# Moving dt's four columns onto z's projection, and the steps of one block's work, in an attention and Mamba kernel on one Trainium2 core

## What is computed

```python
# layer 0
q = einsum('dc,bcn->bnd', wq, xf) + bq; k = einsum('dc,bcn->bdn', wk, xf) + bk[:, None]
attn = softmax(einsum('bnd,bdm->bnm', q, k), axis=-1)
x = gamma * einsum('bcn,bmn->bcm', v, attn) + x            # v likewise
# layer 1
u = layernorm(x as tokens) * norm_g + norm_b
zxbcdt = u @ in_w.T                                        # 256 z, 512 xBC, 4 dt
z, xBC, dt = split(zxbcdt); dt = softplus(dt + dt_bias)
xBC = silu(causal depthwise conv of 4 taps over xBC + conv_b); xs, Bm, Cm = split(xBC)
state = state * exp(dt * A) + (dt * xs) Bm                 # 4 heads of 64, state 128, over tokens
y = (state . Cm + Dp * xs) * silu(z)
out = rmsnorm(y) * rms_w @ out_w.T
x + out * sigmoid(se2 @ relu(se1 @ mean(out) + se1_b) + se2_b)
```

## Time and profile before

| | |
|---|---|
| median of 3 runs | 3152.42 us (3150.59 to 3152.76) |
| the profiled execution | 3150.87 us, its span 3148.70 us |
| PE busy | 2980.0 us, 95% |
| PEld busy | 2322.5 us, 74% |
| DVE busy | 2032.0 us, 65% |
| ACT busy | 1930.0 us, 61% |
| POOL busy | 2009.9 us, 64% |
| mean granted clock of TensorE | 0.983 |

### The profile page before, as it was taken

How to read it: one execution, slowest core, us unless ns; L and a number is a source line. 1 busy time by engine, 2 the same in 40 slices (tenths; PEclk the granted TensorE clock), 3 DMA queues, 4 the chain that set the end, 5 groups by cost and what they waited for, 6 DMA issues and landing times. The chain is left out here.

```text
span 3148.7 us, 63156 instructions
## 1 busy us (share of the span) xinstructions
PE 2980.0 (95%) x21208; PEld 2322.5 (74%) x21208; DVE 2032.0 (65%) x3417; ACT 1930.0 (61%) x3742; POOL 2009.9 (64%) x3087
## 2 busy tenths in 40 slices
PE   6899999999999999999999999999999999999984
PEld 3767777777777777777777777777777777777762
DVE  5556666666666676676676666676666667666654
ACT  2565666666656566666665666666666666666652
POOL 2446666667756576666676656666676667777753
PEclk9999999999999999999999999999999999999986
DMA  3111111111311121222221222122221111212121
GB/s 123 49 37 46 44 51 58 31 54 49 103 63 65 58 71 58 91 77 74 82 77 38 72 76 72 62 76 69 65 89 36 43 49 55 69 50 69 42 95 67
DMA packets 101970, 200.99 MB, mean 64 GB/s; under 512 B 18480, under 2 KB 41392, under 8 KB 97264
## 3 DMA queue, kind: packets, MB, share of 16 engines
q1 hardware_dynamic: 98192, 195.08, 18.6%
q10 hardware_dynamic: 3456, 1.86, 0.2%
HBM read 131.21 MB, written 64.75 MB: 62 GB/s over the span
## 5 line engine op out<-in xcount | busy, mean ns | idle before, releaser
L723 POOL TENSOR_TENSOR p_lo<-p,p_hi 128x512 f16<-128x512 f32 x1024 | 1221.9, 1201 | 845.6 <-ACT p_hi L886 711.9
L879 ACT ACTIVATE p<-p_et 128x512 f32<-128x512 f32 x1024 | 612.2, 598 | 637.4 <-PE p_et L1138 598.0
L1156 PE MATMUL acc<-v_hi,p_hi 128*128 128x257 f16 x4096 | 954.3, 273 | 4.0 <-DVE work L1464 3.8
L1158 PE MATMUL acc<-v_lo,p_hi 128*128 128x256 f16 x4096 | 951.8, 272 | 0.0
L1420 DVE TENSOR_REDUCE maxes<-p_mx 128x1 f32<-128x1024 f32 x508 | 620.1, 1221 | 489.1 <-PE p_mx L1117 488.7
L886 ACT ACTIVATE p_hi<-p 128x512 f16<-128x512 f32 x1024 | 643.5, 629 | 10.0
L1164 PE MATMUL acc<-v_hi,p_lo 128*128 128x257 f16 x4096 | 622.8, 274 | 15.1 <-POOL p_lo L723 15.1
L1156 PEld LDWEIGHTS acc<-v_hi,p_hi 128*128 128x128 f16 x4096 | 399.3, 97 | 125.0 <-issue 54.8
L1158 PEld LDWEIGHTS acc<-v_lo,p_hi 128*128 128x128 f16 x4096 | 400.6, 98 | 117.8 <-issue 49.9
L1164 PEld LDWEIGHTS acc<-v_hi,p_lo 128*128 128x128 f16 x4096 | 399.9, 98 | 68.0 <-POOL p_lo L723 15.9
L1138 PE MATMUL p_et<-qs,kst 98*128 98x256 f16 x2048 | 393.3, 273 | 11.6 <-ACT p L879 11.1
(11 more groups left out here) (213 smaller groups left out, 4164.2 us busy)
## 6 DMA issues: line engine op xcount, KB each, us to landing
work<-rows_d SPq DMA_DIRECT2D x32, 1024.0 KB, 5.2
xin<-in_x_dram SPq DMA_DIRECT2D x48, 512.0 KB, 4.7
xr<-in_x_dram SPq DMA_DIRECT2D x32, 512.0 KB, 3.8
x_d<-x1c SPq DMA_DIRECT2D x31, 512.0 KB, 2.9
og_d<-og SPq DMA_DIRECT2D x29, 512.0 KB, 2.7
mix_x<-x_d SPq DMA_DIRECT2D x25, 512.0 KB, 4.7
mix_o<-og_d SPq DMA_DIRECT2D x24, 512.0 KB, 5.5
out_dram<-mix_o SPq DMA_DIRECT2D x24, 512.0 KB, 2.8
```

Source lines behind the costliest of these rows:

```text
L723: e.tensor_tensor(p_lo[:, n % RING, :], p32[:, n % P32S, :], p_hi[:, n % RING, :], ALU.subtract).then_inc(lo_pool, 1)
L879: e.activation(p32[:, n % P32S, :], p_et[:, :], ACT.Exp).then_inc(exp_done, 1)
L1156: e.matmul(acc[:, t, 0:C + 1], p_hi[:, r, at:at + P], v_hi[:, 2 * k + kk, 0:C + 1], start=(k == 0 and kk == 0), stop=False)
L1158: e.matmul(acc[:, t, 0:C], p_hi[:, r, at:at + P], v_lo[:, 2 * k + kk, :], start=False, stop=False, skip_group_check=True)
```

## The change

- dt has no fill of its own. z is made in four fills of one chunk each, 260 columns wide: 256 of z and dt's 4. Its weights lie in a tensor of their own, inz_sb, loaded with two DMAs; inT_sb keeps the 512 columns of the convolution.
- z's fills are at steps 10, 11, 13 and 15. ScalarE takes the tanh and VectorE adds dt's bias and makes the product, chunk by chunk, in the same steps. zt has two buffers, by block parity, and outputs wait for their own chunk only.
- dt's further work starts at step 15 (K_DT): VectorE 15 and 17, ScalarE 16, softplus on GpSimd 18 to 21, dA still at K_DAT-2, now 22, dAT 24, cumT and decay_rows 26.
- The convolution is at steps 12, 17, 22, 27; the first xsB at 26; the second xT at 19 in place of 30, and with it the next load of xr; the first yn at 26.
- In VectorE's step max_parts is issued right behind the maxima, ahead of stage_b and stage_a.

The diff, cut to its core:

```diff
@@ -47,20 +47,20 @@
 
 
 
-K_X1T, K_UT, K_DT, K_DAT, K_CUM, K_YT, K_OUT = 2, 9, 10, 21, 23, 30, 0
+K_X1T, K_UT, K_DT, K_DAT, K_CUM, K_YT, K_OUT = 2, 9, 15, 24, 26, 30, 0
 K_U = (6, 7)
-K_XBC = (11, 16, 21, 26)
-K_Z = (22, 24)
-K_XSB = (25, 27, 28, 29)
+K_XBC = (12, 17, 22, 27)
+K_Z = (10, 11, 13, 15)
+K_XSB = (26, 27, 28, 29)
 K_SRC = (1, 5, 9, 13)
 K_CB = (2, 6, 10, 14)
 K_Y = (4, 8, 12, 17)
 K_SUM = (6, 10, 14, 19)
 K_SQ = (8, 12, 16, 21)
-K_XT = (13, 30)
+K_XT = (13, 19)
 K_XB = 4
 K_RMS = 22
-K_YN = (27, 28)
+K_YN = (26, 28)
 K_LN = 1
 K_BN = 20
 
...
@@ -128,15 +128,13 @@
             out += [("x1T", A, 0), ("x1T", A, 1)]
         if K == K_UT:
             out += [("uT", A, 0), ("uT", A, 1)]
-        if K == K_DT:
-            out += [("dt", A, 0)]
         if K == K_DAT:
             out += [("dAT", A, 0)]
         if K == K_CUM:
             out += [("cumT", A, 0)]
-        for r in range(2):
-            if K == K_Z[r]:
-                out += [("z", A, r)]
+        for t in range(QT):
+            if K == K_Z[t]:
+                out += [("z", A, t)]
         for c in range(QT):
             if K == K_XSB[c]:
                 out += [("xsB", A, c)]
...
-        inT_sb = sb("inT_sb", [P, CH, 2 * C + 2 * NST + NH])
+        inT_sb = sb("inT_sb", [P, CH, CONVD])
+        inz_sb = sb("inz_sb", [P, CH, C + NH])
...
-        zt = work[:, 5120:6144].rearrange("p (t c) -> p t c", t=QT)
+        zt0 = work[:, 5120:6144].rearrange("p (t c) -> p t c", t=QT)
...
+        zt = [zt0, sb("zt1", [P, QT, C])]
...
-                   (inT_sb[:, :, :], inT.rearrange("(h p) n -> p h n", p=P)),
+                   (inT_sb[:, :, :], inT[:, C:C + CONVD].rearrange("(h p) n -> p h n", p=P)),
+                   (inz_sb[:, :, 0:C], inT[:, 0:C].rearrange("(h p) n -> p h n", p=P)),
+                   (inz_sb[:, :, C:C + NH], inT[:, C + CONVD:C + CONVD + NH].rearrange("(h p) n -> p h n", p=P)),
...
-                e.wait_ge(zs_done, 2 * g + 2)
+                e.wait_ge(zs_done, QT * g + c + 1)
...
@@ -949,13 +950,12 @@
                         e.wait_ge(conv_done, n + 1)
                         wait(e, silu_done, n - 1)
                         e.activation(th[:, m % 2, :], cv, ACT.Tanh).then_inc(tanh_done, 1)
-                for r in range(2):
-                    if K == K_Z[r]:
-                        key = ("z", g, r)
+                for t in range(QT):
+                    if K == K_Z[t]:
+                        key = ("z", g, t)
                         e.wait_ge(filled, n_filled(key))
-                        wait(e, y_ready, g * QT)
-                        e.activation(zt[:, 2 * r:2 * r + 2, :], bank(key)[:, :].rearrange("p (t c) -> p t c", t=2),
-                                     ACT.Tanh, scale=0.5).then_inc(ztanh_done, 1)
+                        wait(e, y_ready, (g - 1) * QT)
+                        e.activation(zt[g % 2][:, t, :], bank(key)[:, 0:C], ACT.Tanh, scale=0.5).then_inc(ztanh_done, 1)
                 for c in range(QT):
                     if K == K_XSB[c]:
                         key = ("xsB", g, c)
...
@@ -1194,20 +1194,12 @@
                 elif name == "uT":
                     e.wait_ge(u_done, 2 * g + 2)
                     turn(key, u, i)
-                elif name == "dt":
+                elif name == "z":
                     e.wait_ge(uT_done, 2 * g + 2)
                     o = begin(key)
-                    for t in range(QT):
-                        for h in range(CH):
-                            mm = e.matmul(o[:, t * NH:(t + 1) * NH], uT[:, h, t * P:(t + 1) * P],
-                                          inT_sb[:, h, C + CONVD:C + CONVD + NH], start=(h == 0), stop=(h == CH - 1))
-                    mm.then_inc(filled, 1)
-                elif name == "z":
-                    o = begin(key)
-                    for t in range(2):
-                        for h in range(CH):
-                            mm = e.matmul(o[:, t * C:(t + 1) * C], uT[:, h, (2 * i + t) * P:(2 * i + t + 1) * P],
-                                          inT_sb[:, h, 0:C], start=(h == 0), stop=(h == CH - 1))
+                    for h in range(CH):
+                        mm = e.matmul(o[:, 0:C + NH], uT[:, h, i * P:(i + 1) * P], inz_sb[:, h, :],
+                                      start=(h == 0), stop=(h == CH - 1))
                     mm.then_inc(filled, 1)
                 elif name == "dAT":
                     o = begin(key)
...
@@ -1487,24 +1479,6 @@
-                if K == K_DT:
-                    key = ("dt", g, 0)
-                    e.wait_ge(filled, n_filled(key))
-                    wait(e, dt_ready, g)
-                    v.tensor_tensor(dtt[:, 0, :].rearrange("p (t h) -> p t h", h=NH),
-                                    bank(key)[:, 0:TH].rearrange("p (t h) -> p t h", h=NH),
-                                    dtb[:, :].unsqueeze(1).to_broadcast([P, QT, NH]), ALU.add).then_inc(dtin_done, 1)
...
@@ -1529,13 +1503,27 @@
                         v.tensor_copy(xbc[:, :, 0:HALO], xbc[:, :, BLK:BLK + HALO]).then_inc(halo_done, 1)
                     else:
                         v.memset(xbc[:, :, 0:HALO], 0.0).then_inc(halo_done, 1)
-                for r in range(2):
-                    if K == K_Z[r]:
-                        key = ("z", g, r)
-                        e.wait_ge(ztanh_done, 2 * g + r + 1)
-                        v.scalar_tensor_tensor(zt[:, 2 * r:2 * r + 2, :], zt[:, 2 * r:2 * r + 2, :], 1.0,
-                                               bank(key)[:, :].rearrange("p (t c) -> p t c", t=2), ALU.add, ALU.mult)\
-                            .then_inc(zs_done, 1)
+                for t in range(QT):
+                    if K == K_Z[t]:
+                        key = ("z", g, t)
+                        e.wait_ge(ztanh_done, QT * g + t + 1)
+                        if t == 0:
+                            wait(e, dt_ready, g)
+                        v.tensor_tensor(dtt[:, 0, t * NH:(t + 1) * NH], bank(key)[:, C:C + NH], dtb[:, :], ALU.add)
+                        v.scalar_tensor_tensor(zt[g % 2][:, t, :], zt[g % 2][:, t, :], 1.0, bank(key)[:, 0:C],
+                                               ALU.add, ALU.mult).then_inc(zs_done, 1)
+                if K == K_DT:
+                    e.drain()
+                    v.scalar_tensor_tensor(dtt[:, 1, :], dtt[:, 0, :], -1.0, dtt[:, 0, :], ALU.mult, ALU.max)\
+                        .then_inc(dtabs_ready, 1)
+                    v.tensor_scalar(dtt[:, 3, :], dtt[:, 0, :], 0.0, None, ALU.max)
+                if K == K_DT + 2:
+                    e.wait_ge(dtexp_done, g + 1)
+                    v.tensor_scalar(dtt[:, 4, :], dtt[:, 2, :], 2.0, None, ALU.add)
+                    e.drain()
+                    v.reciprocal(dtt[:, 5, :], dtt[:, 4, :])
+                    e.drain()
+                    v.tensor_tensor(dtt[:, 4, :], dtt[:, 2, :], dtt[:, 5, :], ALU.mult).then_inc(dtz_ready, 1)
                 if K == K_DAT:
                     key = ("dAT", g, 0)
                     e.wait_ge(filled, n_filled(key))
...
@@ -1623,6 +1611,8 @@
                     for of in pairs_at(*divmod(n, STEPS)):
                         max_pair(*of)
                     h = n // STEPS + 1
+                    if K % STEPS == (K_PARTS if n >= STEPS else K_PARTS_FIRST) and n // STEPS + 1 < NHALF:
+                        max_parts(n // STEPS + 1)
                     if h < NHALF and K % STEPS == (K_QR if n >= STEPS else K_QR_FIRST):
                         query_rows(h)
                 elif s == G and K == 0:
...
@@ -1632,8 +1622,6 @@
                 if 0 <= s - 1 < G:
                     stage_a(s - 1, K)
                 if s < G:
-                    if K % STEPS == (K_PARTS if n >= STEPS else K_PARTS_FIRST) and n // STEPS + 1 < NHALF:
-                        max_parts(n // STEPS + 1)
                     if K == K_BN:
                         bn(0)
                 if (p := proj_at(s, K)) is not None:
```

More of the change, by code:

```diff
@@ L397, in conv_attention_mamba_kernel @@
         uT_done = sem("uT_done")
-        dtin_done = sem("dtin_done")
         dtabs_ready = sem("dtabs_ready")
@@ L480, in emptied @@
                 "out": (og_done, 2 * g + i + 1), "x1T": (x1c_done, 2 * g + i + 1),
-                "uT": (uT_done, 2 * g + i + 1), "dt": (dtin_done, g + 1), "dAT": (dAr_done, g + 1),
-                "cumT": (cum16_done, g + 1), "z": (zs_done, 2 * g + i + 1), "xsB": (xsB_done, QT * g + i + 1),
+                "uT": (uT_done, 2 * g + i + 1), "dAT": (dAr_done, g + 1),
+                "cumT": (cum16_done, g + 1), "z": (zs_done, QT * g + i + 1), "xsB": (xsB_done, QT * g + i + 1),
                 "cb": (mt_ready, QT * g + i + 1), "y": (yt_ready, QT * g + i + 1), "st": (S_ready, QT * g + i + 1),
@@ L814, in outputs @@
                     e.drain()
-                e.wait_ge(zs_done, 2 * g + 2)
+                e.wait_ge(zs_done, QT * g + c + 1)
                 wait(e, filled, n_filled(("yT", g - 1, 1)) if g else 0)
```

(24 more changed lines are left out.)

## The result

The changed kernel takes 3243.59 us (median of 4 runs, 3241.03 to 3248.62) beside 3152.35 before: 1.0292 times as long, 95% interval 1.0275 to 1.031. The forecast was 3153, the range ended at 3182: 91 us more came on than the sum had, and it came in the middle of the kernel. attended() is VectorE's reading of finished values: a reciprocal, a scaling and two products at the head of its step 16 and step 0.

The account below looks back on a forecast made before the run. TensorE, busy 95% of the span, was taken to set the pace while attention runs. Terms -51 -29 +61 +14 +6 = +1 gave 3152 for the profiled execution, 3153 as a median; range 3106 to 3182 for 8 in 10.

Parts of the forecast that it names:

- dt's projection, -51: TensorE: dt's 16 records go, z's get 4 columns wider; 1.65 us saved in each of 31 slots, 51 us off.
- rival C: Step 11: VectorE late at z's bank by 0.3 to 0.6 us in all 31 slots, 3162 to 3172; chance 0.13.
- Waits that go, -29: TensorE's waits for xT, v's second projection, late exponentials and xsB go with the new fill order: 29 us off.
- uT is free earlier: 0, cover is given by whole steps: Among the rest: uT's buffer is released earlier, with whole steps of cover, at a cost of 0.
- The new wait at step 24, +61: ScalarE held at dA by GpSimd's softplus makes TensorE wait for the exponential; 2.55 us in 24 of 31 slots, 61 on.
- second part in step 26: p_lo of tile 26, behind root_mean on GpSimd, comes late for step 26: another 0.45 us a slot.
- The clock, +14: TensorE at 1.2 GHz behind the wait at step 24 in 11 of 24 slots: 14 us on (0 to 31).
- max_parts ahead, 0: Maxima's split moved ahead within VectorE's step; mt of step 6 1 to 2 us later: 0, within 0.2 a slot.
- The end, +6: Behind the last attention step, the chain through dt, softplus, outputs and root_mean lengthens: 6 us on (0 to 8).
- all rivals: Wait at step 24 halved 0.26 or absent 0.08; more slow clock 0.21; VectorE late step 11 0.13; wider matmul failing excluded.

Follow-up runs that it names:

- b_dtone: Kernel before with dt's projection made by one matmul of 16 columns in place of 16 of 4 columns (dt's values wrong): 3103.68 us, 0.9855.
- a_conv16: Kernel after with the second convolution product back in step 16, not 17: 3167.32 us, 1.005.
- b_conv17: Kernel before with the second convolution product in step 17 in place of 16 and nothing else: 3209.22 us, 1.0187.
- a_both: Kernel after with the second convolution product in step 16, and dA, dAT and cumT one step later: 3170.47 us, 1.0061.
- b_dat19: Kernel before with dA's exponential in step 17 in place of 19, dAT and scan in 19, cumT in 21: 3152.21 us, 1.0003.
- f_best: e_pool25 with max_parts behind stage_a again, as in the kernel before: 3105.1 us, 0.985.
- e_pool25: a_both with root_mean on GpSimd alone moved from step 23 to 25, normalisations in 28 and 29: 3112.25 us, 0.9878; run again beside f_best (_b), 3113.6 us, 0.9872.
- e_dtz_parts: e_dtz with max_parts behind stage_a again in VectorE's step: 3134.69 us, 0.9948.
- e_dtz: a_conv16 with dtz's three operations ahead of the convolution's two taps in VectorE's step 17: 3144.25 us, 0.9984.
- c_rms24: a_both with VectorE's guess in step 24, GpSimd's root_mean in 25 and the normalisations in 28 and 29: 3171.35 us, 1.0064.
- c_z14: a_conv16 with z's last part and dt one step earlier (z in 10, 11, 13, 14; softplus in 17 to 20): 3165.03 us, 1.0051.
- d_c16_21: Kernel after with convolution products in steps 12, 16, 21 and 26: 3215.45 us, 1.0198.
- d_rms24_c21: c_rms24 with the third and fourth convolution products one step earlier (12, 16, 21, 26): 3175.2 us, 1.0079.
- d_z14_c21: c_z14 with the convolution products of the kernel before (11, 16, 21, 26): 3194.72 us, 1.0133.
- e_dtz_pool25: e_dtz with root_mean two steps later on GpSimd (25) and the normalisations in 28 and 29: 3145.64 us, 0.9988.

## Why the prediction was wrong, by its own steps

- **dt's projection, -51.** Right in kind and nearly in size. b_dtone measures 47, and TensorE has z in steps 10 to 15 without a wait for VectorE in step 11: rival C did not happen.
- **Waits that go, -29.** xT's 9.9 and vst_lo's 9.0 went, and so did the late exponentials of step 16. xsB's did not go: 6.7 us in place of 0.8, since z no longer stands between the third product and step 26.
- **The product's move from step 16 to 17: no term.** This is the step that failed. The prediction's layout begins at step 17 and adds the convolution's 1.72 us there; the sum has nothing for step 16, from which they are taken. The nearest it comes is "uT is free earlier: 0, cover is given by whole steps", and uT is not free earlier: its last reader, the fourth convolution product, moves from 26 to 27. The prediction never asked what in step 16 the product had covered, although attended() stands at the head of VectorE's step 16 and the values behind the product wait for it. The runs give its price: 51.8 + 7.4 us of waits (the second for p_hi, in six slots) against 1.2, and 76 us of time in a_conv16, clock included. The view of waits from 250 to 3020 us has next to no row for it, because a covered wait has none. The kernel before shows it in two other places. One is the timeline of step 16 (TensorE, then VectorE, whose row holds both products):

```profile
1527.49 1.88 PE L1277 MATMUL p_cv<-work,inT_sb 128*128 128x512 f32 x4
1529.21 0.27 PE L1156 MATMUL acc<-v_hi,p_hi 128*128 128x257 f16 x1
```
```profile
1527.91 0.88 DVE L1464 SCALAR_TENSOR_TENSOR work<-acc,rden,xT 128x256 f32<-128x256 f32 x2
```

  By the trace the first of the two products ends at 1528.40, 0.9 us after the convolution product's start: without it the values would have stood 0.9 to 1.0 us, the 1.0 that b_conv17 measured. The other is step 16 of slot 0, where stage_a does not run and no product stands:

```profile
124.90 0.27 PE L1156 MATMUL acc<-v_hi,p_hi 128*128 128x257 f16 x1 [1.27 <-DVE work L1464]
```

- **The new wait at step 24, +61.** The mechanism, the place and the 24 slots were right; the size was 46.9 us in all, 1.9 a slot for 2.1, and no second part in step 26 (the 0.45 us for it does not follow from the layout either, which has p_lo end at 25.9 and wanted at 25.6). That part was right in kind: it is what a_both laid bare. The prediction did not say that dA's distance alone costs nothing, which b_dat19 showed.
- **The clock, +14.** Too small. It was counted for one wait, and there were two a slot; of the 24 waits at step 24, 12 had a slow stretch behind them, where 11 were taken. TensorE's busy time is 6 us less where the matmuls taken out are 51 less, so some 45 us went to the low clock, 31 more than forecast.
- **max_parts ahead, 0.** It costs 8.5 us (f_best against e_pool25_b) to 9.6 (e_dtz_parts against e_dtz). The waits of mr for yt, 10.1 us for 5.7, and of y for mt, 5.8 new, are its trace; in f_best they are 6.2 and none among the larger ones, with xw at 13.7.
- **The end, +6.** The last energies and the span:

```profile
L1138 PE MATMUL p_et<-qs,kst x2048: 270/272/421, 52.5 to 3113.3; 98*128 98x256 f16 x187
```

  3246.5 - 3113.3 = 133.2 us behind them; before, 3148.7 - 3022.6 = 126.1. It is +7.

Put together against the forecast of +1: 58 for attended and p_hi, 31 for the clock, about 14 less for the exponential, about 13 for mt, yt, xsB and xw, 1 at the end: 89 of the 91 us that were missing. That these add up so closely is partly luck, since each is read from one execution. The clock's and the small waits' shares are worked out from rows, not measured alone. The range failed because all rivals lay within the same list of moved things; none was "a cover is lost".

## What to carry to other kernels

When work of the engine that sets the pace is moved from one step to another, it is not free even if the sum of the steps is the same: list, for the step that it leaves, everything that the instructions behind it wait for, and how long ago its maker could start. A covered wait has no row in the view of waits; the timeline shows it, as the time at which its maker ends beside the start of the work that covers it. And when a wait is removed and the time stays, read the next wait before giving up the theory. Against the wait at step 24, six placements (a_both, c_rms24, c_z14, d_c16_21, d_rms24_c21, d_z14_c21) moved the loss to other queues in whole or in part, once through the edit's own neighbour on VectorE; two (e_dtz, e_dtz_pool25) took about half of it; and the one that freed the queue which had become the next in line (e_pool25, GpSimd's root_mean with its normalisations) was faster than the kernel before.

## What the runs showed of the hardware

**The clock falls behind waits of 2 us.** Behind the wait of 2.07 us at 1558.46 the granted clock is 0.53 in the next 3.5 us, and behind the 1.75 us at 1580.97 it is 0.68: part of each at 1.2 GHz. Not every such wait does it: of the 24 waits for attended() at step 16 from 250 us on, 10 have a part at 1.2 GHz in the next 3.5 us, of the 24 at step 24, 12; of the six of 1.24 us for p_hi, none. The Trainium skill, "TensorE: Matmul & The Clock Gate", in "Why this matters for your kernels", asks for no idle gaps over about 3 us between bursts of matmuls. The trace does not bear that out as a safe bound here: both waits are shorter, and the measurement decides.

**A small VectorE instruction is held by GpSimd's p_lo.** L1517, on 128x16 elements, over the whole execution (duration ns min/median/max):

```profile
L1517 DVE SCALAR_TENSOR_TENSOR dtt<-dtt x32: 175/958/970, 207.0 to 3159.5; 128x16 f32<-128x16 f32 x32
```

The one shown above ended at 1557.28, and GpSimd's pair of p_lo ran from 1554.98 for 2.27 us, to 1557.25. So it is throughout: 25 of the 32 meet a p_lo and end 0.03 us behind its end, and the seven that meet none take 0.175 us. The guess of c_rms24 did the same, 0.77 and 1.04 us beside a p_lo and 0.17 behind it. The Trainium skill, "GPSIMD Engine Reference", in Specifications, has GpSimd's SBUF interfaces shared with VectorE, with contention where VectorE's instruction has two SBUF inputs or uses both ports. The trace agrees for L1517, which has two inputs. It adds a size that the section does not give: 0.8 us a time for 16 columns, and this lies in the middle of the wait for attended().
